# Attention scores on 64-row stacks and two row tiles, and an exponential with a constant bias

## What is computed

```python
q = x @ Wq
latent_kv = (x @ Wk + x @ Wv) @ W_down_kv
k_rec, v_rec = latent_kv @ W_up_k, latent_kv @ W_up_v
scores = einsum('bhqd,bhkd->bhqk', heads(q), heads(k_rec)) / sqrt(128)
scores = scores * exp(-0.0001 * abs(i - j))
out = einsum('bhqk,bhkd->bhqd', softmax(scores), heads(v_rec))
```

## Time and profile before

| | before |
|---|---|
| median of 3 runs | 1060.61 us (1056.14 to 1063.99) |
| span of the profiled execution, first to last instruction | 1054.7 us |
| PE (TensorE) busy | 1006.9 us, 95% |
| DVE (VectorE) busy | 808.3 us, 77% |
| ACT (ScalarE) busy | 804.5 us, 76% |
| POOL (GpSimd) busy | 235.8 us, 22% |
| mean granted TensorE clock | 0.990 |
| moved by DMA | 188.98 MB, mean 179 GB/s |

### The profile page before, as it was taken

One profiled execution on the slowest core, in us unless ns is written; L12 is line 12 of the kernel. 1 busy time (PEld: TensorE's weight loads), 2 busy tenths in 40 slices (PEclk: granted clock), 3 DMA queues, 4 the chain that ended last, 5 costly groups with the idle time before them and its releaser, 6 DMA issues.

```text
span 1054.7 us, 20344 instructions
## 1 busy us (share of the span) xinstructions
PE 1006.9 (95%) x5274; PEld 681.7 (65%) x5274; DVE 808.3 (77%) x1837; ACT 804.5 (76%) x1356; POOL 235.8 (22%) x371
## 2 busy tenths in 40 slices
PE   5799999999997999999999999999998998999997
PEld 3333333333335688888888888888884887788885
DVE  8644444444448799999999999999995788699997
ACT  5799999999996787887887877878875553855554
POOL 3776765554463000000000000000005112300000
PEclk9799999999999999999999999999999999999999
DMA  4477876777651587767777777777731000034331
GB/s 134 144 230 238 256 253 219 230 231 229 223 202 40 178 310 248 238 235 240 238 245 240 245 233 239 245 241 245 245 107 60 1 2 1 1 128 125 115 95 40
DMA packets 102991, 188.98 MB, mean 179 GB/s; under 512 B 11932, under 2 KB 56604, under 8 KB 102940
## 3 DMA queue, kind: packets, MB, share of 16 engines
q1 hardware_dynamic: 102756, 188.19, 55.0%
q10 hardware_dynamic: 192, 0.30, 0.1%
HBM read 152.46 MB, written 35.98 MB: 179 GB/s over the span
## 4 chain that ended last, share of the span: by engine, by line
PE 86%; DVE 4%; ACT 4%; DMA 2%; POOL 1%; issue 1%; SPq 0%; DVEq 0%; ACTq 0%; POOLq 0%
PE bank L1483 28%; PE bank L1496 16%; PE bank L1381 12%; PE bank L1490 8%; PE bank L1365 6%; PE bank L1362 6%; PE bank L1581 1%; PE bank L1392 1%; PE bank L1204 1%; DVE state L2056 1%; POOL rstd L690 1%; PE bank L1591 1%; DVE stats L1705 1%; ACT xn L882 1%; PE bank L1586 1%
## 5 line engine op out<-in xcount | busy, mean ns | idle before, releaser
L1483 PE MATMUL bank<-xh,w_parts 128*128 128x512 f32 x896 | 276.6, 390 | 2.2 <-ACT xn L1131 1.3
L983 ACT ACTIVATE ring<-bank,minus_bound 128x1024 f32<-128x1024 f32 x256 | 263.0, 1118 | 13.9 <-PE bank L1365 9.0
L1082 ACT ACTIVATE bank<-bank 128x512 f32<-128x512 f32 x320 | 186.2, 582 | 88.8 <-PE bank L1483 88.8
L1970 DVE TENSOR_TENSOR bank<-bank,ring 128x512 f32<-128x512 f32 x320 | 223.9, 700 | 25.3 <-DMA ring<-c_rows 2.4
L1496 PE MATMUL bank<-hh,w_parts 128*128 128x512 f32 x772 | 238.1, 390 | 0.0
L1962 DVE TENSOR_TENSOR hl<-bank,hh 128x512 fp32r<-128x512 f32 x321 | 218.5, 681 | 0.1
L1862 DVE TENSOR_TENSOR bank<-bank,corner 128x128 f32<-128x128 f32 x256 | 76.4, 299 | 154.9 <-PE bank L1365 153.8
L1483 PEld LDWEIGHTS bank<-xh,w_parts 128*128 128x128 f32 x896 | 167.3, 188 | 39.0 <-DVEq L1956 1.7
L1076 ACT ACTIVATE hh<-bank 128x512 fp32r<-128x512 f32 x321 | 190.4, 593 | 1.0 <-DVE bank L1970 0.9
L1483 PE MATMUL bank<-xl,w_parts 128*128 128x512 f32 x448 | 174.4, 389 | 0.0
L1496 PEld LDWEIGHTS bank<-hh,w_parts 128*128 128x128 f32 x772 | 144.9, 188 | 30.5 <-ACT hh L1076 0.8
(11 more groups left out here) (324 smaller groups left out, 1137.8 us busy)
## 6 DMA issues: line engine op xcount, KB each, us to landing
ring<-c_rows SPq DMA_DIRECT2D x173, 512.0 KB, 4.7
w_parts<-w_pairs SPq DMA_DIRECT2D x160, 128.0 KB, 2.9
w_pairs<-xh SPq DMA_DIRECT2D x16, 768.0 KB, 4.4
q_stack<-q_parts SPq DMA_DIRECT2D x63, 144.0 KB
k_stack<-k_parts SPq DMA_DIRECT2D x189, 48.0 KB
w_pairs<-xl SPq DMA_DIRECT2D x16, 512.0 KB, 2.9
big<-in_w_exp SPq DMA_DIRECT2D x16, 384.0 KB, 4.9
w_ffn_parts<-xl SPq DMA_DIRECT2D x16, 384.0 KB, 3.8
```

Source lines behind the costliest of these rows:

```text
L983: act.activation(ring[:, c % RING * S:(c % RING + 1) * S], wide[(m + c) % SB][:], ACT.Exp, bias=minus_bound[:]).then_inc(exp_done, 1)
L1082: act.activation(bank(4 + c % ZB), bank(4 + c % ZB), ACT.Silu).then_inc(silu_ready, 1)
L1483: ins = pe.matmul(out_, w[i], x_[j], start=start and k == 0, stop=stop and k == 2, skip_group_check=not start)
L1970: dve.tensor_tensor(bank(4 + c % ZB), bank(4 + c % ZB), cb[u][:, g * GW:(g + 1) * GW], ALU.mult).then_inc(hid_ready, 1)
```

## The change

The pairs of parts go from 9 to 8 (the product of the two smallest is left out), so that a side has 64 rows instead of 72. Side-wise stacks are replaced: rows 0 to 63 of a q stack hold queries of the first half (0 to 511), rows 64 to 127 those of the second, with side 0 in columns 0 to 511 and side 1 in columns 512 to 1023. The k stack holds in both halves of the rows the same 64 rows, with side 0 in columns 0 to 1023 and side 1 behind it (4 KB per row). A score piece of query half h is contracted over the 64 rows of that half, so the two halves of a tile use different row tiles of the matrix unit. No rows are left unfilled, so the memsets go. DRAM has one tensor each for q and k with both sides in a line. The bias is the constant -40 (`BOUND`), which `flag` has already been compared with; `minus_bound`, its matmul and its VectorE operation go. SyncE waits for `first_half` instead of `whole`, because that is now counted last. `hid`, a tile of the experts' stage that shared memory with a stack, gets its own.

```diff
-PAIRS = 9
+PAIRS = 8
+ROWS = PAIRS * HD
...
-        q_stack = [[sb(f"q_stack{s}{u}", [P, S], BF16) for u in range(2)] for s in range(2)]
-        k_stack = [[sb(f"k_stack{s}{u}", [P, S], BF16) for u in range(2)] for s in range(2)]
+        q_stack = [sb(f"q_stack{u}", [P, S], BF16) for u in range(2)]
+        k_stack = [sb(f"k_stack{u}", [P, 2 * S], BF16) for u in range(2)]
+
+        def q_rows(u, v, h, lo, hi):
+
+            return q_stack[u][h * ROWS:(h + 1) * ROWS, v * 512 + lo:v * 512 + hi]
+
+        def k_rows(u, v, h, lo, hi):
+
+            return k_stack[u][h * ROWS:(h + 1) * ROWS, v * S + lo:v * S + hi]
...
-        q_dram = [dram(f"q_parts{s}", [NH, 3, HD, S], BF16) for s in range(2)]
-        k_dram = [dram(f"k_parts{s}", [NH, HD, 3, S], BF16) for s in range(2)]
+        q_dram = dram("q_parts", [NH, 3, HD, 2, 2, GW], BF16)
+        k_dram = dram("k_parts", [NH, HD, 3, 2, S], BF16)
...
-        def load_stack(eng, n, u, v):
-
-            eng.dma_start(q_stack[v][u][0:PAIRS * HD, :], bass.AP(q_dram[v].tensor, n * (3 * HD * S), [[S, 3 * HD], [0, 3], [1, S]]))\
-                .then_inc(stacks_loaded[u], 16)
-            for i in range(3):
-                eng.dma_start(k_stack[v][u][i * 3 * HD:(i + 1) * 3 * HD, :],
-                              bass.AP(k_dram[v].tensor, n * (3 * HD * S), [[S, 3 * HD], [1, S]])).then_inc(stacks_loaded[u], 16)
+        line, head_lines = 2 * S, 3 * HD * 2 * S
+
+        def load_q(eng, n, u):
+
+            for h in range(2):
+                for row, rows, first_line, lines, copies in ((0, 48, 0, 16, 3), (48, 16, 16, 8, 2)):
+                    eng.dma_start(q_stack[u][h * ROWS + row:h * ROWS + row + rows, :],
+                                  bass.AP(q_dram.tensor, n * head_lines + first_line * line + h * S,
+                                          [[line, lines], [0, copies], [1, S]])).then_inc(stacks_loaded[u], 16)
+
+        def load_k(eng, n, u):
+
+            for h in range(2):
+                eng.dma_start(k_stack[u][h * ROWS:h * ROWS + 48, :],
+                              bass.AP(k_dram.tensor, n * head_lines, [[0, 2], [line, 3 * HD], [1, line]])).then_inc(stacks_loaded[u], 16)
+                eng.dma_start(k_stack[u][h * ROWS + 48:(h + 1) * ROWS, :],
+                              bass.AP(k_dram.tensor, n * head_lines, [[3 * line, HD], [line, 2], [1, line]])).then_inc(stacks_loaded[u], 16)
...
-                                       bias=minus_bound[:]).then_inc(exp_done, 1)
+                                       bias=-BOUND).then_inc(exp_done, 1)
...
-                    for j, h in enumerate((k // 4, 1 - k // 4)):
-                        lo, hi, mid = h * 512, (h + 1) * 512, min(max(k * P, h * 512), (h + 1) * 512)
-                        if mid > lo:
-                            ins = pe.matmul(wide[(m + c) % SB][:, lo:mid], k_stack[0][u][:, keys], q_stack[1][u][:, lo:mid],
-                                            start=True, stop=True)
-                        if hi > mid:
-                            ins = pe.matmul(wide[(m + c) % SB][:, mid:hi], k_stack[1][u][:, keys], q_stack[0][u][:, mid:hi],
-                                            start=True, stop=True)
-                        ins.then_inc((first_half, whole)[j], 1)
+                    tile, own, at = wide[(m + c) % SB], k // 4, k % 4 * P
+
+                    def part(h, v, lo, hi):
+
+                        return pe.matmul(tile[:, h * 512 + lo:h * 512 + hi], k_rows(u, v, h, k * P, (k + 1) * P), q_rows(u, 1 - v, h, lo, hi),
+                                         start=True, stop=True)
+
+                    if at:
+                        part(own, 0, 0, at)
+                    part(1 - own, 1 - own, 0, 512).then_inc(whole, 1)
+                    part(own, 1, at, 512).then_inc(first_half, 1)
...
-            for u in range(2):
-                for v in range(2):
-                    for stack in (q_stack, k_stack):
-                        ins = dve.memset(stack[v][u][:], 0.0)
```

More of the change, by code:

```diff
@@ L58 @@
 CREDIT = 2
+SAVES = 2 * 8
 class Link:
@@ L213, in ffn_parts @@
             return [w_parts[:, u * 6 * D + (3 * k + j) * D:u * 6 * D + (3 * k + j + 1) * D] for k in range(2)]
-        act_out = [q_stack[0][u][:].bitcast(F32) for u in range(2)]
-        shared_hid = act_out + [k_stack[0][u][:].bitcast(F32) for u in range(2)]
-        shared_z = [k_stack[1][u][:].bitcast(F32) for u in range(2)] + [evac[u][:] for u in range(2)]
-        hid = [q_stack[1][u][:].bitcast(F32) for u in range(2)]
+        act_out = [q_stack[u][:].bitcast(F32) for u in range(2)]
+        shared_hid = act_out + [k_stack[u][:, 0:S].bitcast(F32) for u in range(2)]
+        shared_z = [k_stack[u][:, S:2 * S].bitcast(F32) for u in range(2)] + [evac[u][:] for u in range(2)]
+        hid = [sb(f"hid{u}", [P, GW])[:] for u in range(2)]
         hh = [sb(f"hh{u}", [P, GW], F32R) for u in range(2)]
@@ L514, in _, with load_stacks, q_rows_of @@
                 load_raw(0, u)
-            def load_stacks(n, u, sides=(0, 1)):
-                for v in sides:
-                    load_stack(sp, n, u, v)
-            def rows_of(drams, g, w):
-                return drams[w][g // 2 * H:(g // 2 + 1) * H, :, :, g % 2 * GW:(g % 2 + 1) * GW]
+            def load_stacks(n, u):
+                load_q(sp, n, u)
+                load_k(sp, n, u)
+            def q_rows_of(g, i):
+                return q_dram[g // 2 * H:(g // 2 + 1) * H, i, :, g % 2, :, :]
             def store_k(g, w, part, saved):
-                sp.dma_start(rows_of(k_dram, g, w).rearrange("h d i t -> (h d) i t"), part).then_inc(saved, 16)
+                sp.dma_start(k_dram[g // 2 * H:(g // 2 + 1) * H, :, :, w, g % 2 * GW:(g % 2 + 1) * GW].rearrange("h d i t -> (h d) i t"), part).then_inc(saved, 16)
             for g in range(2):
@@ L1258, in _ @@
             pe.transpose(bank(5)[0:1, 0:H], bound[0:H, 4:5], ident[0:H, 0:H]).then_inc(bound_psum, 1)
-            pe.wait_ge(bound_root, 1)
-            pe.matmul(bank(6)[:, 0:1], ones[0:1, :], bound[0:1, 1:2], start=True, stop=True).then_inc(bound_psum, 1)
             def projection(g):
@@ L1728, in low_x @@
                 dve.tensor_tensor(xl[:, cols], xnT[:, cols], xh[:, cols].bitcast(F32), ALU.subtract).then_inc(xl_ready, 1)
-            for u in range(2):
-                for v in range(2):
-                    for stack in (q_stack, k_stack):
-                        ins = dve.memset(stack[v][u][:], 0.0)
-                        if (u, v, stack) != (1, 1, k_stack):
-                            link.sign(ins)
-            link.wait()
-            ins.then_inc(stacks_zero, 1)
             norm(0)
```

28 lines of the change are left out of this document (10 added, 18 removed).

## The result

The changed kernel takes 1208.55 us (1205.85 to 1211.62), beside 1058.38 us of the kernel before on the same chip: 1.143 times as long, with a 95% interval of 1.140 to 1.147. The prediction was 1222 us (1175 to 1325). The profiled execution has a span of 1209.9 us, 155 us more than before; its own time, 1211.62 us, is the longest of the four.

A forecast was written before the change was run, and what follows sets the result against it. TensorE and ScalarE bound the kernel before, within 4%; afterwards two DMA engines would. Attention ending at 475 us instead of 313.6 adds 161 to the 1054.7 us span, giving 1216, plus 5.9 makes 1222 us (range 1175 to 1325).

The forecast's parts named there:

- The two engines: Stack loads: each 48-row k load, source repetition 2 outermost, can only be cut in two, 24 lines of 4 KB per engine.
- The price per head: Attention heads: the two busiest engines carry 8.3 us of k loads, 1.6 other loads, 3.4 weights; 13.3 us against ScalarE's 8.0.
- the sum: Attention: 32 heads x 9.9 us, 30 heads' weights x 3.4, late stores 8.3: 427 us from 37.6 us; attention ends at 475.
- The 1 us to report: End of attention: 1 us between the last head's load landing at 465 us and its eight tiles, which take 9 us.
- 1.6 us for the other loads: Per head: the two busiest engines' share of the six loads besides the 48-row ones, 37 KB, takes 1.6 us.
- Signs foretold: Profile after: heads about 13 us apart, 5 us PE waits, ACT idle some 150 us, 68 small packets, DMA share about 0.4.
- Scores side by side: Attention scores on two row tiles: could save 0.213 us per tile, PE dropping to 6.6 to 7.5 us per head.
- The bias: Attention exponentials: constant bias saves nothing to 0.06 us per tile, 0 to 15 us over 256, if ScalarE is the bound.
- Spread widely: Rival, stack loads: 48-row loads on 6 engines or more, 7.6 to 8.0 us per head, 1048 us; chance 0.07.
- SyncE's issues: Rival, load queue: eight loads at 0.83 us to issue make 9.2 us per head, +29 us, 1089 us; chance 0.03.
- Nothing gained: Rival, attention: loads spread, but halves not side by side or switches cost it; PE still 8.3 us per head, 1060 us; chance 0.05.
- Start-up: Start: removed memsets, small product and VectorE operation are worth nothing, lying beside loads that end later.

The follow-up runs named there:

- the first experiment: The changed kernel with each 48-row load of k cut into two loads of 24 rows, ten loads per head instead of eight: 1087.13 us, ratio 1.028.

## Why the prediction was right, point by point

**The two engines.** The step that carried the forecast, that the load of 48 rows is cut along the outermost step of both sides and so in two, is shown four times: by the packets (11036, exact), by the 49 GB/s slices, by the time that comes back when the load is split, and in the kernel before by three engines for a repetition of three. The trace of before did not choose between the two cuts; taking this one was my own estimate. Two more counts agree: the four loads of ScalarE's queue before are 144 lines and 192 packets, so 12 small ones each, and with 30 of the 48-row loads left out 10976 small packets remain, 11036 - 30 x 2.

That the small packets stand for engines is in the traces too. The small packets from 42 to 310 us are all of 4 bytes in their records, 4656 before and 2484 after. And the packets of lines that are open at the same moment, in the time from 45 to 330 us when nothing but lines of that size is open, are most often as many as the small ones of a load:

| loads, their outermost counts | run | small packets per load | open at once, for how long in all |
|---|---|---|---|
| k, source 2, target 48 | changed kernel | 2 | 2, 69.9 us |
| k, source 3, target 72 | one wide load in the kernel before | 3 | 3, 36.3 us |
| k, 24; k, source 8, target 16 | each cut into two of 24 rows | 12; 8 | 12, 18.0 us; 8, 12.2 us |

For these four kinds of load the number is the largest up to 16 that divides both outermost counts; for others it is not shown.

**The price per head.** 13.3 us were worked out from 23.6 GB/s per engine; measured are 24.5 GB/s and heads 12.7 us apart. 13.3 x 23.6 / 24.5 is 12.8. So the rate was a little too low, and the terms together come to what was measured. Over the sum's 427 us this rate alone would take off 16 us, but the attention ended only 9 us before the forecast's 475. The other 7 came back in terms that were too small: the first score starts at 51.58 us, where the sum has 37.6 + 9.9 + 1 = 48.5 (48.1 at the measured rate); the last head takes 10.9 us for its eight tiles (454.88 to 465.8), not 9, as the products of its first two pairs run at 1.93 us; the rest, under 2 us, lies among the 31 heads between, which with the late stores are 13.0 us apart on average. The 1 us to report is shown by no run: in the chain above the load lands at 222.01 us and TensorE starts at 222.05. One part of the 1.6 us for the other loads, 25 of the 37 KB or 1.0 us, needs that the 8 engines of a 16-row load include the two. No run shows this directly; while only packets of 4 KB were open in the changed kernel, eight at once make 1.45 us and ten 0.01 us, which fits it.

**From the span to the time.** The sum gives a span of 1216 us, measured is 1209.9: 9 us less for the attention and 3 us more behind it, at a clock of 0.99 instead of 1.00. On top of the span the prediction put 5.9 us, the distance between the median of the kernel before and the span of its profiled execution. That distance is for the most part no property of a kernel: an execution's own time exceeds its span by 1.7 us (1211.62 against 1209.9), and the rest is how the profiled execution stands among the others. Here it was the longest, so the median lies 1.4 us under its span. That is 7 of the 13.5 us by which 1222 was too high.

**Signs foretold.** PE's wait at a head's start is 3.2 to 4.3 us in the heads shown, 4.2 on average (5 foretold), ScalarE idles 185 us (150), small packets per head are 68, as foretold, and the DMA share is 0.47 (0.4; I had left out that the stretch also holds the late stores and the start). The 25 us that the prediction's range sets aside for a slow clock are shown by no run. The clock was granted at 0.50 from 209.33 to 214.00 us, behind a wait of 4.28 us, and at 0.78 on average over the attention: the products of two tiles, 1.06 us elsewhere, took 1.93 us in the first two pairs after a wait. It costs little, since the loads are what ends last, with heads 12.7 us apart where 13.3 were forecast.

**The first two edits.** Scores side by side: 0.21 us per tile, shown. TensorE's head without waits is two pairs with turns at 2.01 us (measured, and 2.44 less 0.43) and two without at an estimated 1.97 - 0.43 = 1.54, together 7.1 us, inside the 6.6 to 7.5. The bias: exponentials of a head start (4.69 - 1.02) / 4 = 0.92 us apart, less than the 0.95 to 1.00 that I had taken. The bound of 0.06 us per tile from the casts was too low: from start to start the constant gives 1.00 - 0.92 = 0.08 us, and in duration 85 to 97 ns. Why the casts, without a bias operand in the profile, take longer than these exponentials is not shown.

**The rivals.** "Spread widely" had a threshold of 6 engines and 1048 us. With 12 engines the first experiment came out at 1087, so that rival was wrong about its own case: what failed is that I had put the engines' load and SyncE's issues into two rivals, with 0.07 for the one and 0.03 for the other. Once the engines were no longer the bound, the issues were, at 9.5 us per head for ten loads where 9.2 had been worked out for eight. "Nothing gained" is answered by the scores side by side and by heads of 7.33 us. With both out of the way the gain is 1.0 us per head, not the 0.4 that the rival had. Start-up: the first loads are issued at 35.82 us (35.93 before), so the memsets were indeed worth nothing.

## What to carry to other kernels

Before a load is given a repetition as its outermost step, count over how many engines it can be cut: an outermost count of 2 left 14 of 16 engines without a share of it here (DMA share 0.13, 50 GB/s), at the same bytes and with fewer loads to issue. Then add up the issue times of the queue per turn of the loop, since the next bound here, 9.5 us of issues per head, lay above the 8.3 us of the kernel before and kept the first remedy 32 us slower than it. And where two engines are within a few per cent of each other, a faster step on one of them is worth nothing until the other gets one too: here 0 and 0.3 us per head apart, 1.0 together.

## What the runs showed that I had not expected

- The time of an issue on SyncE depends on more than the number of steps: four q loads took 2.71 us in the changed kernel, 3.27 and 3.68 with the full queue of the first experiment. A full queue is not the reason, or not alone: with one load left out they took 3.23 us right after the queue had waited for TensorE, and 3.25 to 3.60 with the k loads on ScalarE, where SyncE's queue waited 112 of 200 us. The cause stays open.
- An issue on ScalarE's queue takes 0.36 to 0.85 us of ScalarE itself; six of them hold the next exponential up for 3.7 to 4.3 us (two heads seen).
- On one row tile, 64-row scores next to full 128-row transposes cost 0.25 us per pair of tiles more than 128-row scores do, next to products of 32 columns nothing.
- A store whose source repeats its lines two or three times is dearer to issue: 6 in 7.95 us instead of 4.88.
- TensorE's clock stayed at 0.50 while TensorE was busy. With one row tile it was granted at 1.00 from 60 to 80 us; then TensorE waited 3.6 us for a load (its scores went on at 87.70 us), and from 90 to 140 us the clock was 0.50 although TensorE was busy for all 50 us, the scores of two tiles taking 1.88 us instead of 1.04 and their products 1.93 instead of 1.07. From 150 us on it was 1.00 again, with the same work. With both row tiles a wait of 5.85 us at the same place (scores from 81.90 us) was followed by slow products in two pairs only. The runs don't tell what makes the difference.
